# Score products of two attentions at full depth, each head's keys alone among zeros

## What is computed

```python
# layer 0, causal (att0); q, k, v with a low-rank addition to the weights
att = einsum('bhqd,bhkd->bhqk', q, k) / sqrt(8)
att = softmax(where(causal, att, -inf)); y = einsum('bhqk,bhkd->bhqd', att, v)
# inside layer 0's feed-forward part, not causal (att1)
scores = einsum('bqhd,bkhd->bhqk', q, k) / sqrt(8)
ctx = einsum('bhqk,bkhd->bqhd', softmax(scores), v)
```

## Time and profile before

| | us |
|---|---|
| median of 3 runs | 1055.25 |
| lowest, highest | 1051.7, 1070.48 |
| the profiled execution | 1069.91 |
| its span, first to last instruction | 1068.1 |
| mean granted TensorE clock in it | 0.890 |

### The profile page before, as it was taken

How to read it: one execution, slowest core, us unless ns; L and a number is a source line. 1 busy time by engine, 2 the same in 40 slices (tenths; PEclk the granted TensorE clock), 3 DMA queues, 4 the chain that set the end, 5 groups by cost and what they waited for, 6 DMA issues and landing times.

```text
span 1068.1 us, 19608 instructions
## 1 busy us (share of the span) xinstructions
PE 980.0 (92%) x6830; PEld 768.5 (72%) x6830; DVE 615.1 (58%) x1489; ACT 536.1 (50%) x1144; POOL 99.3 (9%) x169
## 2 busy tenths in 40 slices
PE   5999988999999999999998799979999788888888
PEld 3666557888888888888887466648999665555665
DVE  4455437556666555666653565433222499999684
ACT  3553335555555555555551465435444366666441
POOL 1011010000000000000001000000000154444100
PEclk9775569999999999999999566559999999999997
DMA  6000000000000000000001000000110000000000
GB/s 247 2 2 1 1 1 2 1 2 1 0 0 0 0 0 0 0 0 0 0 0 41 0 2 2 1 10 21 40 39 29 0 2 1 0 0 0 8 13 21
DMA packets 6555, 12.96 MB, mean 12 GB/s; under 512 B 496, under 2 KB 2544, under 8 KB 6128
## 3 DMA queue, kind: packets, MB, share of 16 engines
q1 hardware_dynamic: 6512, 12.38, 3.5%
HBM read 11.85 MB, written 0.52 MB: 12 GB/s over the span
## 4 chain that ended last, share of the span: by engine, by line
PE 77%; DVE 12%; issue 5%; ACT 4%; DVEq 1%; POOL 1%; DMA 1%; SPq 0%; ACTq 0%
PE psum L893 8%; PE psum L905 8%; PE psum L1027 6%; PE psum L873 4%; PE psum L875 4%; PE psum L874 4%; PE psum L865 4%; DVE arena L1735 4%; PE psum L624 4%; PE psum L604 3%; PE psum L570 3%; PE psum L858 3%; PE psum L1011 2%; PE psum L1012 2%; PE psum L1013 2%
## 5 line engine op out<-in xcount | busy, mean ns | idle before, releaser
L1858 DVE TENSOR_REDUCE xnegmax<-psum 128x1 f32<-128x768 f32 x128 | 122.4, 956 | 138.7 <-PE psum L875 138.5
L1408 ACT ACTIVATE arena<-psum,xnegmax 128x768 f32<-128x768 f32 x128 | 115.4, 902 | 138.9 <-DVE xnegmax L1858 97.5
L893 PE MATMUL psum<-pack_a,arena 128*128 128x128 f32 x768 | 106.9, 275 | 0.2 <-ACT arena L1399 0.2
L873 PE MATMUL psum<-kv_high,xq_high 128*128 128x384 f32 x256 | 101.3, 396 | 1.7 <-DVE kv_low L1853 1.6
L893 PEld LDWEIGHTS psum<-pack_a,arena 128*128 128x128 f32 x768 | 87.3, 141 | 13.9 <-issue 12.3
L1399 ACT ACTIVATE arena<-psum 128x512 f32<-128x512 f32 x128 | 75.9, 593 | 42.5 <-PE psum L893 42.5
L905 PE MATMUL psum<-arena,xv 128*64 128x256 f32 x768 | 90.0, 384 | 0.0
L1224 ACT ACTIVATE pT<-psum 128x768 f32<-128x768 f32 (+1 forms) x64 | 58.8, 918 | 58.8 <-PE psum L608 39.1
L875 PE MATMUL psum<-kv_high,xq_low 128*128 128x384 f32 x256 | 86.8, 339 | 0.0
L874 PE MATMUL psum<-kv_low,xq_high 128*128 128x384 f32 x256 | 86.6, 338 | 0.0
L1618 DVE TENSOR_REDUCE negmax<-psum 128x6 f32<-128x768 f32 (+1 forms) x64 | 68.3, 1088 | 29.1 <-PE psum L575 18.0
(11 more groups left out here) (276 smaller groups left out, 1916.0 us busy)
## 6 DMA issues: line engine op xcount, KB each, us to landing
w1b<-in_w SPq DMA_DIRECT2D x9, 256.0 KB, 2.7
w2b<-in_w SPq DMA_DIRECT2D x9, 256.0 KB, 2.7
pack_v<-in_pack_v SPq DMA_DIRECT2D x1, 1088.0 KB, 9.1
pack_l<-in_pack_l SPq DMA_DIRECT2D x1, 1079.5 KB, 12.0
pack_q<-in_pack_q SPq DMA_DIRECT2D x1, 1024.0 KB, 6.9
pack_a<-in_pack_a SPq DMA_DIRECT2D x1, 649.5 KB, 6.2
x<-in_x SPq DMA_DIRECT2D x2, 256.0 KB, 3.2
arena<-in_mask SPq DMA_DIRECT2D x1, 512.0 KB, 3.7
```

The costliest lines, as they stand in the source:

```text
L873: mm(out, xq_high[:, u % 2, tile], kv_high[:, u // 2, keys], start=True, stop=False)
L893: last = transpose(bank[4 + (3 * u + c) % 2][:, (2 * i + h) * P:(2 * i + h + 1) * P], xprob[:, u % 2, h * KEYS + kt * P:h * KEYS + (kt + 1 ...
L1408: activation(xprob[:, u % 2, half * KEYS:(half + 1) * KEYS].rearrange("p (c w) -> p c w", c=2), src, ACT.Exp, bias=xnegmax[:, u % 2, half: ...
L1858: v.tensor_reduce(xnegmax[:, u % 2, half:half + 1], banks_pair(half), AX.XY, ALU.max, negate=True)\
```

## The change

GpSimd gets, for every group, four products of kslot with a column of the new constant slotmask (1 in the 32 rows of one head, 0 elsewhere) and writes them to kalone. The score products of both kinds take the whole qslot or qshift and the head's kalone, at depth 128, instead of 32 rows of each. So that GpSimd has time, spread and slots run one more step ahead, and kslot has two buffers, qslot four, kalone three. The scores of a group wait for all four of its heads (`alone`). In att0 the four context jobs of POOL are placed behind the keys of groups 6, 8, 10 and 12; before, POOL's queue held them ahead of everything else. The spread matrix is loaded into z2 in place of a buffer of its own.

```diff
-            spread_in = at("spread_in", [P, PARTS * P])
-            qslot, kslot = at("qslot", [P, 3, T], f32r), at("kslot", [P, 3, T], f32r)
+            qslot, kslot = at("qslot", [P, 4, T], f32r), at("kslot", [P, 2, T], f32r)
+            kalone = at("kalone", [P, 3, HG, T], f32r)
...
                     if p == 0:
                         a.wait(pe, "slot_ready", it + 1)
+                        a.wait(pe, "alone", HG * it + HG)
...
-                            last = mm(bank[SCORE_BANKS[p][k]][:, out], qslot[r, it % 3, u * P:(u + 1) * P],
-                                      kslot[r, it % 3, 0:keys], start=(u == 1 or not a.causal), stop=not a.causal,
+                            last = mm(bank[SCORE_BANKS[p][k]][:, out], qslot[:, it % 4, u * P:(u + 1) * P],
+                                      kalone[:, it % 3, 2 * p + k, 0:keys], start=(u == 1 or not a.causal), stop=not a.causal,
                                       skip_group_check=True)
...
-                            last = mm(bank[4 + k][:, out], kslot[r, it % 3, kt * P:(kt + 1) * P], qshift[r, queries],
+                            last = mm(bank[4 + k][:, out], kalone[:, it % 3, 2 * p + k, kt * P:(kt + 1) * P], qshift[:, queries],
...
                 spread_slots(0, 2)
+                spread_slots(1, 7)
                 for i in range(STEPS):
...
-                    if i + 1 < GROUPS:
+                    if i + 2 < GROUPS:
                         if i == 0 and a is att1:
                             pe.wait_ge(x_done, 4)
                         evacuated(i - 1)
-                        spread_slots(i + 1, 1)
+                        spread_slots(i + 2, 1)
...
-                    if i + 1 < GROUPS:
-                        a.wait(pe, "slot_ready", i + 2)
+                    if i + 2 < GROUPS:
+                        a.wait(pe, "slot_ready", i + 3)
...
                 def slots(it, bk):
                     a.wait(act, "spread_psum", it + 1)
-                    if it >= 3:
-                        a.wait(act, "st_psum", 2 * it - 4)
-                    activation(kslot[:, it % 3, :], bank[bk][:, T:2 * T], ACT.Identity, bias=col("a", "unit_rows"))
-                    activation(qslot[:, it % 3, :], bank[bk][:, 0:T], ACT.Copy).then_inc(heads["slot_ready"], 1)
+                    if it >= 2:
+                        a.wait(act, "alone", HG * (it - 2) + HG)
+                    activation(kslot[:, it % 2, :], bank[bk][:, T:2 * T], ACT.Identity, bias=col("a", "unit_rows"))\
+                        .then_inc(heads["kslot_ready"], 1)
+                    if it >= 4:
+                        a.wait(act, "shift_psum", it - 3)
+                    activation(qslot[:, it % 4, :], bank[bk][:, 0:T], ACT.Copy).then_inc(heads["slot_ready"], 1)
...
                 slots(0, 2)
+                slots(1, 7)
                 square_jobs(after_zT)
...
+            def keys_alone(a):
+                for it in range(GROUPS):
+                    a.wait(pool, "kslot_ready", it + 1)
+                    if it >= 3:
+                        a.wait(pool, "st_psum", 2 * (it - 3) + 2)
+                    for j in range(HG):
+                        pool.tensor_tensor(kalone[:, it % 3, j, :], kslot[:, it % 2, :],
+                                           col("a", "slotmask")[:, j:j + 1].broadcast_to([P, T]), ALU.mult)\
+                            .then_inc(heads["alone"], 1)
+                    if a is att0:
+                        for c, step in enumerate((6, 8, 10, 12)):
+                            if it == step:
+                                rstd_jobs([("ctx", c)])
...
             rstd_jobs(FIRST_JOBS)
-            rstd_jobs(CONTEXT_JOBS[0])
-            rstd_jobs(CONTEXT_JOBS[1])
+            keys_alone(att0)
             rstd_jobs([("n1", 0), ("n1", 1), ("lat", 0), ("lat", 1)])
             cross()
...
             rstd_jobs([("n2", 1), ("ln1", 1)])
+            keys_alone(att1)
             rstd_jobs([("ln2", 0), ("ln2", 1)])
```

More of the change, by code:

```diff
@@ L62 @@
 LAYOUT = {
-    "a": [("ident", P), ("unit_rows", 1), ("headmask", H), ("causal", P), ("la0", D), ("lb0", 3 * D), ("w0", 3 * D),
+    "a": [("ident", P), ("unit_rows", 1), ("slotmask", HG), ("headmask", H), ("causal", P), ("la0", D), ("lb0", 3 * D), ("w0", 3 * D),
           ("bq0", 1), ("bk0", 1), ("bv0", D)],
@@ L301, in decoder @@
             COUNTS = {"zT_psum": 2, "zT_act": 2, "qk_psum": 4, "high": 4, "low": 4, "v_psum": 2, "v_ready": 2,
-                      "spread_psum": GROUPS, "slot_ready": GROUPS,
+                      "spread_psum": GROUPS, "slot_ready": GROUPS, "kslot_ready": GROUPS, "alone": HG * GROUPS,
                       "s_psum": 2 * GROUPS, "max_done": 2 * GROUPS, "w_ready": GROUPS, "shift_psum": GROUPS,
@@ L451, in _ @@
             sp.dma_start(packs["a"][:, :], packs_d["a"]).then_inc(loaded["a"], 16)
-            sp.dma_start(spread_in[:, :], spread_d).then_inc(loaded["s"], 16)
+            sp.dma_start(quarter(z2, 0), spread_d.rearrange("p (a c) -> p a c", a=PARTS)).then_inc(loaded["s"], 16)
             sp.dma_start(ctx_x[:, :, :], ctx_d.rearrange("b (u p) c -> p (b u) c", p=P)).then_inc(loaded["ctx"], 16)
@@ L564, in scores @@
                         for k in range(2):
-                            r = slice(ROWS * (2 * p + k), ROWS * (2 * p + k + 1))
                             if a.causal:
@@ L583, in shifted @@
                         a.wait(pe, "yU_ready", it - 1)
-                    mm(bank[0][:, 0:T], identr[:, :], qslot[:, it % 3, :], start=True, stop=False, skip_group_check=True)
+                    mm(bank[0][:, 0:T], identr[:, :], qslot[:, it % 4, :], start=True, stop=False, skip_group_check=True)
                     for i in range(2):
@@ L669, in head_attention @@
                             a.wait(pe, "v_ready", 1)
+                            a.wait(pe, "slot_ready", 2)
                         scores(i, 1)
-                    if i + 1 < GROUPS:
+                    if i + 2 < GROUPS:
                         if i == 0 and a is att1:
@@ L1257, in head_attention @@
                         exponentials(i - 1, 0)
-                    if i + 1 < GROUPS:
-                        slots(i + 1, 1)
+                    if i + 2 < GROUPS:
+                        slots(i + 2, 1)
                     if i >= 2:
@@ L1505, in _ @@
             act.wait_ge(loaded["s"], 16)
-            activation(spread_of[:, :, :], spread_in[:, :].rearrange("p (a c) -> p a c", a=PARTS), ACT.Copy).then_inc(constants, 1)
+            activation(spread_of[:, :, :], quarter(z2, 0), ACT.Copy).then_inc(constants, 1)
             for u in range(2):
@@ L2283, in _arrange @@
         "ident": np.eye(P, dtype=np.float32),
+        "slotmask": (np.arange(P)[:, None] // ROWS == np.arange(HG)[None]).astype(np.float32),
         "unit_rows": np.isin(np.arange(P) % ROWS, SHIFT_ROWS).astype(np.float32).reshape(P, 1),
```

## The result

The changed kernel is slower: 1087.6 us in the median (1085.46 to 1092.3, 4 runs) against 1060.68 us for the kernel before on the same chip, a ratio of 1.029 (95% interval 1.019 to 1.039). Medians are of all runs; a ratio compares, on one chip, the runs of each kernel that lie within 1.5% of its fastest. The forecast was 1057 us: 1087.6 lies inside its range of 1032 to 1090, at the upper end, but the sum forecast 7.9 us less and the trace shows 22.4 more, so the sign is wrong and the size too. The profiled execution of the changed kernel took 1092.3 us, its span is 1090.5 us, 22.4 us over the span before.

What follows compares the result with a forecast made beforehand. TensorE was taken to set the pace, at half clock in much of att0 and att1. att0 +7.8, att1 -14.2 and tails -1.5 us gave -7.9, so 1062.0 in the profiled execution's terms, lowered to 1057 us; range 1032 to 1090.

Steps and rivals of the forecast that it cites:

- the clock rises with depth: att0 and att1: nearly all busy steps run at full clock after one or two slow steps at their start.
- the four waits: att0, steps 6, 8, 10, 12: PE waits for keys queued behind POOL's context jobs, 2 x 5.3 + 2 x 3.5 = 17.6 us.
- such a fall after each of the four waits: att0: PE's clock falls to half after each wait for keys, 2 us each, 8 in all (0 to 14).
- (d): att0: whole steps stay at half clock until the next wait, four times 5 us instead of 2, 1069 us; chance 0.10.
- that batch: att1: twelve products issued together at full clock; full depth makes them 0.3 us dearer per step.
- The bound of 1.8 us a step: Upper bound on the price of full depth on PE: 16 products x 0.11 us, if now all were hidden.
- the guess of 0.45: att0: full depth costs 0.45 us a step, as half of the products have only 128 columns and weight loads show more.
- the starts: First scores wait for four keys: att0 2.5 us later, att1's first L584 3.7 us late; att1's slow steps +3.5.
- the level: Whole kernel: profiled execution lies 14.7 us above the median; a third kept as still to be lost, 1062.0 to 1057 us.
- (a): att0 and the starts: the clock holds through the waits and rises at once, 1045 us; chance 0.18.
- (b): att0: the context jobs don't hold PE, as DVE gets to them earlier than read, 1031 us; chance 0.09.
- (c): att0 and att1: the clock doesn't follow depth, so nothing is won and each part is paid, 1104 us; chance 0.15.

Runs made afterwards that it cites:

- the run with the later jobs: The changed kernel with each of POOL's four context jobs in att0 one group later (behind the keys of groups 7, 9, 11, 13): 1052.5 us, ratio 0.991.
- the run with row tiles: The changed kernel, all waits and buffers kept, but each score product again takes only the head's 32 rows: 1099.4 us, ratio 1.034 to the kernel before.
- the version with depth everywhere: The changed kernel with context jobs one group later and the spread products also at full depth: 1040.9 us, ratio 0.988 to the kernel before.

## Why the prediction was wrong

**Right:** what bounds the kernel (PE at half clock); that the clock rises with depth; the mechanism, place and length of the four waits (17.6 us forecast, 17.4 measured); att0's steps at full clock. Without the waits the steps 7 to 16 take 51.0 us in the run with the later jobs, and 50.6 were forecast.

**The step that failed most: "I expect such a fall after each of the four waits and take 2 us for each, 8 in all (0 to 14)."** It is 20.6 us, 5 us a wait, over the upper bound given, and 12.6 of the 16 us that att0's steps missed. The mechanism was there, the size wasn't: no row gave the 2 us, and the row named beside it has 20.5 us of half clock after a gap, another 61.4 us of it with PE never at rest. Those rows say that in att0's mix of products a low clock can last long; they were read as a matter of row tiles alone. In the changed kernel the pieces last 10 to 20 us. Rival (d), "falls after the waits are long", had exactly this at 4 x 5 us and stood at a chance of 0.10.

**Second: "So that batch costs 12 x 0.11 - 0.99 = 0.3 us more per step."** The batch costs 1.95 - 0.99 = 0.96 us more, and a whole common step of att1 at full clock 5.04 - 4.31 = 0.73. The distance was taken from a stretch in which nothing changes (L865); full-depth products with 256 columns stand 0.12 us apart, and the four of L536, still from 32 rows, stand between eight from 128 and cost two changes. The bound of 1.8 us a step held it. In att1 13 steps at full clock took (715.26 - 648.45) / 13 = 5.14 us where 4.7 was forecast, 5.7 us in all. In att0 the guess of 0.45 came out nearly, at 0.54 (the third to the seventh step at full clock take 28.45 us with the later jobs, 25.77 before), with a batch that is dearer than thought: that was luck.

**Third: the starts.** att1's two slow steps took 7.8 and 8.2 us, 16.0 together where 2 x 4.7 + 3.5 = 12.9 was forecast: the clock came back only at 647.2. Its first L585 was 5.0 us late, not 3.7. The keys came when forecast (the first score 14.8 us after the transposes); what was mis-sized is behind them, from the first score to the first L585: 5.0 us (627.37 to 632.42) where 3.5 was forecast. Ahead of that L585, PE also issues a spread, waits 0.84 us for ACT's copies of it (L1218) and issues group 1's first scores; the forecast counted none of these. att0's first score came 2.8 us late, as forecast, and its first L585 4.5. att0's first step stayed at half clock and took 9.2 us, where 7.6 was measured before and the forecast's terms give some 7. The timeline shows the chain forecast for att1's keys:

```profile
621.74 0.65 ACT L1189 ACTIVATE squares<-centred 128x512 f32<-128x512 f32 x1
...
623.48 1.01 POOL L2169 TENSOR_TENSOR stat<-stat,half 128x4 f32<-128x4 f32 x1
...
624.45 5.06 POOL L2179 TENSOR_TENSOR kalone<-kslot,pack_a 128x256 fp32r<-128x256 f32 x8
624.52 1.09 DVE L1574 TENSOR_TENSOR z<-centred,stat 128x512 f32<-128x512 f32 x1 [1.41 <-POOL stat L2169]
```

**Fourth: the level.** The sum itself has a slip of 0.2 us (start, slow steps and depth give +2.0 at step 7, not +1.8), which changes nothing. From the sum of 1062.0 the text went down to 1057, as if the changed kernel shared the profiled execution's distance from the median. The changed kernel's runs lie within 7 us of each other and its profiled one is 4.7 us above the median; the correction made the miss larger.

**The rivals.** (a), the clock holds through the waits, and (b), the jobs don't hold PE, are refuted by the timeline. (c), the clock doesn't follow depth, is refuted by the run with row tiles; its 1104 us is 16 us over the measured time, (d)'s 1069 19 us under it, so the time alone couldn't have told them apart. Its mark, a clock of 0.50 in att1, is absent. (d) was right in its mechanism and size; the dearer steps and the level are what it lacked.

## What to carry to other kernels

When a job is put into the queue of an engine that has just become part of the main chain, ask what it waits for and what stands behind it; one position later cost nothing here and gained 35 us. A gap of PE costs more than its length if the clock falls with it: take the time to come back from the same stage's own rows, and not from a guess. And if products go to full depth, move their neighbours too: a few row tiles between full-depth products lose the overlap and pay for the change, twice.

## What was not expected of the hardware

- Four products a step at full depth, in place of 32-row ones, lifted the mean granted clock of att0 from 0.64 to 0.92 in the profiled executions, with the rest of the attention as before. The two halves of the scores are not equal in cost: with the transposed scores deep instead of the scores, the last 13 steps of att1, at full clock in both, take 63.9 us against 60.3.
- With row tiles the granted clock differs from execution to execution: the kernel before had single times from 1033 to 1077 us, with mean clocks from 0.939 down to 0.881; the version with depth everywhere had 1037.3 to 1042.4 us and 0.952 to 0.957.
- GpSimd can hold DVE up. DVE's L1574, with two inputs in SBUF, takes 0.69 us otherwise and 1.09 us at 624.52, where POOL's key products had started at 624.45. The Trainium skill ("SBUF — State Buffer", Who interferes with whom) says that a DVE instruction with two SBUF inputs contends with a GpSimd instruction that reads SBUF; the row agrees (0.40 us longer, less than one key product of 0.617). In the steady steps little of it is seen: DVE's L1642 has a mean of 0.20 us in att1, 0.18 before.
